# Differential attention with all keys of a slot in one run, token sums in two buffers, values one slot later and the output product in the middle of the next pair

## What is computed

```python
def _L1_attn_ref(x, Wq, Wk, Wv, Wo, lq1, lk1, lq2, lk2):
    h, dh = (16, 64)
    q = (x @ Wq).reshape(B, S, 2, h, dh)
    k = (x @ Wk).reshape(B, S, 2, h, dh)
    v = (x @ Wv).reshape(B, S, 2, h, dh)
    ...
    s1 = jnp.einsum('bshd,bthd->bhst', q1, k1) * scale
    s2 = jnp.einsum('bshd,bthd->bhst', q2, k2) * scale
    ...
    a1 = jax.nn.softmax(s1, axis=-1)
    a2 = jax.nn.softmax(s2, axis=-1)
    o = jnp.einsum('bhst,bthd->bshd', a1, v1) - lam * jnp.einsum('bhst,bthd->bshd', a2, v2)
    o = o.reshape(B, S, h * dh) * (1.0 - LAMBDA_INIT)
    return o @ Wo
x = _layernorm(x + _L1_attn_ref(x, ...), axis=-1)
```

## Time and profile before

| | us |
|---|---|
| three runs: lowest, median, highest | 1697.77, 1699.48, 1701.35 |
| the profiled execution: device time | 1697.64 |
| its span from first to last instruction | 1695.9 |
| PE busy in the span | 1608.2 (95%) |
| DVE, ACT, POOL busy in the span | 1187.9, 910.8, 676.7 (70%, 54%, 40%) |

### The profile page before, as it was taken

How to read it: one execution, slowest core, us unless ns; L and a number is a source line. 1 busy time by engine, 2 the same in 40 slices (tenths; PEclk the granted TensorE clock), 3 DMA queues, 4 the chain that set the end, 5 groups by cost and what they waited for, 6 DMA issues and landing times. The chain is left out here.

```text
span 1695.9 us, 51949 instructions
## 1 busy us (share of the span) xinstructions
PE 1608.2 (95%) x18158; PEld 1339.1 (79%) x18158; DVE 1187.9 (70%) x3418; ACT 910.8 (54%) x2619; POOL 676.7 (40%) x1070
## 2 busy tenths in 40 slices
PE   7998999897999999999999999899999999999695
PEld 5777788786777777777777777799999999999564
DVE  6888888675776677767676776467777777777654
ACT  5776777642454445444554454565655656565241
POOL 3665666411233333333333333234444344444346
PEclk9999999998999999999999999999999999999898
DMA  3213211121231000001110000112212212122231
GB/s 94 65 42 109 76 56 56 48 57 37 52 71 28 25 25 25 25 25 29 28 29 25 25 25 25 40 49 53 61 40 61 57 44 61 45 56 57 74 99 45
DMA packets 157654, 82.30 MB, mean 49 GB/s; under 512 B 17641, under 2 KB 153115, under 8 KB 157568
## 3 DMA queue, kind: packets, MB, share of 16 engines
q1 hardware_dynamic: 154800, 77.68, 17.2%
q0 software_dynamic: 2048, 3.15, 0.6%
q10 hardware_dynamic: 720, 0.33, 0.1%
HBM read 61.03 MB, written 21.27 MB: 49 GB/s over the span
## 5 line engine op out<-in xcount | busy, mean ns | idle before, releaser
L1437 PE MATMUL bank<-diff_xT,diff_w_score 128*128 128x128 f32 x2048 | 259.5, 280 | 0.8 <-ACT diff_xT L1549 0.8
L1437 PEld LDWEIGHTS bank<-diff_xT,diff_w_score 128*128 128x128 f32 x2048 | 242.1, 193 | 22.4 <-issue 20.2
L1556 ACT ACTIVATE diff_keys<-bank 128x512 f32<-128x512 f32 x256 | 152.4, 595 | 165.9 <-PE bank L1437 165.9
L1746 POOL TENSOR_TENSOR diff_prob<-diff_prob,diff_inv_sum 128x512 f32<-128x512 f32 x64 | 67.2, 1050 | 380.5 <-DVE diff_inv_sum L1649 380.5
L2225 POOL TENSOR_TENSOR lat_prob<-lat_prob,lat_inv_sum 128x512 f32<-128x512 f32 x128 | 133.5, 1043 | 208.3 <-DVE lat_inv_sum L2150 207.3
L2025 ACT ACTIVATE lat_prob<-bank,lat_neg_max 128x128 f32<-128x128 f32 x512 | 180.5, 372 | 1.0 <-DVE lat_neg_max L2170 1.0
L2036 ACT ACTIVATE lat_query<-bank 128x512 f32<-128x512 f32 x128 | 76.5, 597 | 174.4 <-PE bank L1920 174.4
L1950 PE MATMUL bank<-lat_catT,lat_query 128*128 128x128 f32 x1024 | 142.4, 282 | 3.9 <-ACT lat_query L2036 3.9
L1920 PE MATMUL bank<-lat_catT,lat_w_score 128*128 128x128 f32 x1024 | 139.5, 280 | 2.3 <-ACT lat_catT L2017 1.0
L1950 PEld LDWEIGHTS bank<-lat_catT,lat_query 128*128 128x128 f32 x1024 | 125.2, 193 | 15.8 <-issue 10.6
L1930 PE MATMUL bank<-lat_probT,lat_c_rep 32*128 32x256 f32 x2048 | 130.0, 391 | 3.1 <-DVE lat_z L2155 3.1
(11 more groups left out here) (273 smaller groups left out, 3656.6 us busy)
## 6 DMA issues: line engine op xcount, KB each, us to landing
lat_c_rep<-cat SPq DMA_DIRECT2D x128, 128.0 KB
stage<-low_y SPq DMA_DIRECT2D x64, 64.0 KB, 1.6
diff_x_rep<-stage SPq DMA_DIRECT2D x128, 32.0 KB, 1.8
lat_c_t<-cat SPq DMA_DIRECT2D x32, 128.0 KB, 2.2
exp_w<-in_L_ffn_w_dram SPq DMA_DIRECT2D x16, 256.0 KB, 3.0
expert_rows<-latw_zeros SPq DMA_DIRECT2D x4, 548.0 KB, 5.4
exp_rows<-expert_rows SPq DMA_DIRECT2D x8, 274.0 KB, 3.9
low_x_t<-in_x_dram SPq DMA_DIRECT2D x32, 64.0 KB, 1.9
```

The source lines that it names most:

```text
L1437: last = nc.tensor.matmul(ring[(k + d) % 2][:, j * P:(j + 1) * P], w_score[:, H1 * (k // 2) + HS * d + 4 * (k % 2) + j, :], xT[:, :], star ...
L1556: nc.scalar.activation(keys[:, k // 2, 4 * (k % 2):4 * (k % 2) + 4, :].rearrange("p h t -> p (h t)"), ring[(k + d) % 2][:, :], ACT.Copy).t ...
```

## The change

It reorders the work of a slot, and gives `mix` a second buffer. No matmul, copy or transfer is added or removed.

1. The four key banks of a slot stand in one run on PE; the mixes follow, then the values. On ACT the copies of banks 2 and 3 come before the copies of `mix`.
2. `mix` gets a leading dimension of 2, indexed by `d`. The values of slot `n - 3` run in slot `n`, where they were those of slot `n - 2`. They go into `ring[d]` as before, now with the heads of the other slot kind.
3. The output product moves from the end of slot d = 1 to the end of slot d = 0 of the following pair, from `ring[1]` to `ring[0]`. `z` moves to slot d = 1, and `y`, `lat` and their statistics and powers move by half a pair or more on DVE and POOL.
4. On DVE the copies of `mix` move behind the sums of the softmax (`mix_copies`), just ahead of the transpose (`turn`).
5. On SP the load of `x_rep` moves ahead of that of `x_res`; the stores of `y` and `lat` are for pair `i - 3`. One more round of `pair` drains the pipeline, and a transpose of a bias for the next phase uses `bank[1]` in place of `bank[0]`.

The core of the diff (the moves on DVE and POOL are cut to their heads):

```diff
-        mix = sb("mix", [P, 4, HS, 2, L])
+        mix = sb("mix", [P, 2, 4, HS, 2, L])
...
-            for i in range(NPAIR - 2, NPAIR + 2):
+            for i in range(NPAIR - 2, NPAIR + 3):
...
+                if have(i):
+                    wait(sp, mix_done, 2 * (i - 1))
+                    load_rep(i, par)
...
-                if have(i, 2):
-                    sp.wait_ge(y_done, i - 1)
-                    sp.dma_start(rows(x_out, i - 2), y[:, :]).then_inc(y_stored, 16)
-                if have(i, 2):
-                    sp.wait_ge(lat_done, i - 1)
-                    store_cat(i - 2, S, lat, lat_stored)
+                if have(i, 3):
+                    sp.wait_ge(y_done, i - 2)
+                    sp.dma_start(rows(x_out, i - 3), y[:, :]).then_inc(y_stored, 16)
+                if have(i, 3):
+                    sp.wait_ge(lat_done, i - 2)
+                    store_cat(i - 3, S, lat, lat_stored)
...
-                            tokens = mix[:, att:4 - att:3 - 2 * att, 2 * t + par, :, :].rearrange("p f b l -> p b f l")
+                            tokens = mix[:, d, att:4 - att:3 - 2 * att, 2 * t + par, :, :].rearrange("p f b l -> p b f l")
                             last = nc.tensor.matmul(
-                                ring[d][par * HD1:(par + 1) * HD1, t * P:(t + 1) * P]
+                                ring[1 - d][par * HD1:(par + 1) * HD1, t * P:(t + 1) * P]
...
+                    valued = have(i, 2) if d == 0 else have(i, 1)
                     if have(i):
                         if d == 0:
                             pe.wait_ge(xT_ready, i + 1)
-                            key_bank(n, d, 0, k_copied, 4 * n)
+                        key_bank(n, d, 0, k_copied, 4 * n)
+                        if d == 0:
+                            key_bank(n, d, 1, o_copied, n - 3)
+                        else:
                             key_bank(n, d, 1, z_done, i - 1)
-                        else:
-                            key_bank(n, d, 0, k_copied, 4 * n)
-                            key_bank(n, d, 1, o_copied, n - 2)
+                        key_bank(n, d, 2, k_copied, 4 * n + 1)
+                        key_bank(n, d, 3, k_copied, 4 * n + 2)
                     if have(i, 1):
                         pe.wait_ge(rep_loaded[1 - par], 32 * (i + par) if isinstance(i, int) else 32 * i + 32 * par)
                         mixes(n - 2, d, 1 - par)
...
-                    if have(i):
-                        key_bank(n, d, 2, k_copied, 4 * n + 1)
-                        key_bank(n, d, 3, k_copied, 4 * n + 2)
-                    if have(i, 1):
+                    if valued:
                         if have(i):
                             pe.wait_ge(k_copied, 4 * n + 3)
+                        elif d == 0:
+                            wait(pe, z_done, i - 2)
                         else:
-                            wait(pe, o_copied, n - 3)
-                        values(n - 2, d)
+                            wait(pe, o_copied, n - 4)
+                        values(n - 3, 1 - d)
...
-                    if d == 1 and have(i, 1):
-                        pe.wait_ge(o_copied, 2 * i)
+                    if d == 0 and have(i, 2):
+                        pe.wait_ge(o_copied, 2 * (i - 1))
                         for t in range(HS):
-                            last = nc.tensor.matmul(ring[1][:, 0:D], oT[:, t // 4, t % 4, :], wo[:, t, :],
+                            last = nc.tensor.matmul(ring[0][:, 0:D], oT[:, t // 4, t % 4, :], wo[:, t, :],
                                                     start=(t == 0), stop=(t == HS - 1))
                         last.then_inc(wo_done, 1)
...
+                    if have(i):
+                        copy_keys(n, d, 2)
+                        copy_keys(n, d, 3)
                     if have(i, 1):
                         act.wait_ge(mix_done, n - 1)
-                        wait(act, o_done, n - 2)
+                        wait(act, o_done, n - 3)
                         for q in range(2):
-                            nc.scalar.activation(mix[:, q % 2::2, :, q // 2, :],
+                            nc.scalar.activation(mix[:, d, q % 2::2, :, q // 2, :],
                                                  ps_mix[q][:, :].rearrange("p (f h l) -> p f h l", f=2, h=HS), ACT.Copy)\
                                 .then_inc(mix_act, 1)
                     if isinstance(i, int) and i == NPAIR:
                         latent.copies(act, (0, 1) if d == 0 else (4, 5))
-                    if have(i):
-                        copy_keys(n, d, 2)
-                        copy_keys(n, d, 3)
-                    if have(i, 1):
-                        act.wait_ge(o_done, n - 1)
-                        if d == 0:
+                    if have(i, 2) if d == 0 else have(i, 1):
+                        act.wait_ge(o_done, n - 2)
+                        if d == 1:
                             wait(act, wo_done, i - 1)
-                        nc.scalar.activation(oT[:, d, :, :].rearrange("p t e -> p (t e)"), ring[d][:, :], ACT.Copy)\
+                        nc.scalar.activation(oT[:, 1 - d, :, :].rearrange("p t e -> p (t e)"), ring[d][:, :], ACT.Copy)\
                             .then_inc(o_copied, 1)
...
+            def mix_copies(n, d):
+                dve.wait_ge(mix_done, n + 1)
+                wait(dve, o_done, n - 1)
+                for q in range(2, 4):
+                    nc.vector.tensor_copy(mix[:, d, q % 2::2, :, q // 2, :],
+                                          ps_mix[q][:, :].rearrange("p (f h l) -> p f h l", f=2, h=HS)).then_inc(mix_dve, 1)
+            def turn(n, d):
+                dve.wait_ge(p_done, 2 * (n + 1))
+                wait(dve, mix_done, n - 1)
+                nc.vector.transpose(probT[:, d, :], prob[:, d, :]).then_inc(pT_done, 1)
...
-                    if d == 0 and have(i, 2):
+                    if d == 0 and have(i, 3):
+                        dve.wait_ge(rstd_done[0], i - 2)
+                        wait(dve, y_stored, 16 * (i - 3))
+                        nc.vector.tensor_scalar(y[:, :], z[:, :], mean_var[:, 0, 0:1], rstd[:, 0:1], ALU.subtract,
+                                                ALU.mult).then_inc(y_done, 1)
+                    if d == 1 and have(i, 2):
                         dve.wait_ge(res_loaded, 16 * (i - 1))
                         dve.wait_ge(wo_done, i - 1)
-                        nc.vector.scalar_tensor_tensor(out=z[:, :], in0=ring[1][:, 0:D], scalar=1.0 - LAMBDA,
+                        nc.vector.scalar_tensor_tensor(out=z[:, :], in0=ring[0][:, 0:D], scalar=1.0 - LAMBDA,
                                                        in1=x_res[:, :], op0=ALU.mult, op1=ALU.add).then_inc(z_done, 1)
-                    if d == 1 and have(i, 2):
-                        dve.wait_ge(rstd_done[0], i - 1)
-                        wait(dve, y_stored, 16 * (i - 2))
-                        nc.vector.tensor_scalar(y[:, :], z[:, :], mean_var[:, 0, 0:1], rstd[:, 0:1], ALU.subtract,
-                                                ALU.mult).then_inc(y_done, 1)
+                    if d == 1 and have(i, 3):
+                        dve.wait_ge(rstd_done[1], i - 2)
+                        wait(dve, lat_stored, 32 * (i - 3))
+                        nc.vector.tensor_scalar(lat[:, :], y[:, :], mean_var[:, 1, 0:1], rstd[:, 1:2], ALU.subtract,
+                                                ALU.mult).then_inc(lat_n_done, 1)
...
+                    if have(i, 1):
+                        mix_copies(n - 2, d)
                     if done:
-                        dve.wait_ge(p_done, 2 * n)
-                        wait(dve, mix_done, n - 2)
-                        nc.vector.transpose(probT[:, 1 - d, :], prob[:, 1 - d, :]).then_inc(pT_done, 1)
+                        turn(n - 1, 1 - d)
...
-                        if have(i, 2):
-                            power(0, i - 1)
+                        if have(i, 3):
+                            power(1, i - 2)
                         if have(i):
                             power(2, i + 1)
                     else:
-                        if have(i, 2):
-                            power(1, i - 1)
+                        if have(i, 3):
+                            scale_shift(lat, 2, lat_n_done, lat_g_done, lat_done, i - 2)
                         if have(i):
                             scale_shift(ctx_n, 0, ctx_n_done, ctx_g_done, ctx_done, i + 1)
                         if have(i, 2):
-                            scale_shift(lat, 2, lat_n_done, lat_g_done, lat_done, i - 1)
+                            power(0, i - 1)
```

More of the change, by code:

```diff
@@ L1273, in products @@
         pe.wait_ge(self.r_loaded, 32)
-        nc.tensor.transpose(self.core.bank[0][:, 0:self.NB1], self.b1_raw[:, :], self.core.ident[0:self.NB1, 0:self.NB1])\
+        nc.tensor.transpose(self.core.bank[1][:, 0:self.NB1], self.b1_raw[:, :], self.core.ident[0:self.NB1, 0:self.NB1])\
```

(23 more changed lines are left out.)

15 lines of the change are left out of this document (6 added, 9 removed).

## The result

The changed kernel takes 1724.23 us (median of four runs, 1719.36 to 1728.32) against 1700.41 of the kernel before (1697.77 to 1702.05): 1.0143 times over the runs (the two medians alone give 1.0140), 95% interval 1.0116 to 1.0171. The profiled execution took 1719.36 us, its span is 1717.6 us, 21.7 us longer than that of before. The forecast was 1718, with 1708 to 1727 as its range.

What follows compares the result with a forecast made beforehand. PE was taken as the bound. Moved product +18.9, key run outrunning ACT +14.3, fewer shape changes -13.3, drain waits -1.3 sum to +18.6 us: median 1718 us against 1699.5, range 1708 to 1727.

Runs made afterwards that it cites:

- e7: Changed kernel with two `xT` buffers, exponentials behind key bank 1's copy, and the output product between key banks 1 and 2 of slot d = 1: 1687.21 us, 0.9932.
- e4: Kernel before the change with one of the output product's eight matmuls kept, so output is incomplete: 1704.32 us in one run, a loop pair still 19.98 us.
- e2: Changed kernel with key banks 2 and 3 put behind the mixes again, and their ACT copies likewise: 1722.34 us, 1.0115 of the kernel before.
- e3: Changed kernel with both exponentials on ACT placed behind the copy of key bank 1: 1722.99 us, 1.0117 of the kernel before.
- e5: The kernel of e4 with DVE taking `z` ahead of the softmax subtraction: 1659.6 us in one run, output still incomplete.

## What to carry over

An instruction group that is moved away takes its cover along: list what other engines do under it (here ACT's `xT` copy and DVE's `z`) and give each another cover or a second buffer before moving it. When a kernel's bound engine is busy all the time, its waits hide between starts; compare the distance of starts with the undisturbed pitch, and look in the warm-up for the order that the change will make. A group of the same weight shape is a cheap filler for a wait in a run: in e7 the product in the run of keys cost no change of shape and hid the copies.

## What the hardware showed

Changing the weights' shape costs PE start-to-start time: about 0.1 us to leave 128 x 128 weights (sixteen keys ahead of mixes 1.88 us, ahead of more keys 1.79), 0.1 us to enter them behind 32-row weights (0.38 against 0.28 for the first), 0.05 to enter 64-column ones (0.33 against 0.28). Taking 1.56 us of 19.97 from the engine that was busy 100% of the time changed nothing in the pairs of the loop (e4), since two waits of 0.22 and 0.86 us took its place, with the lengthened first keys.

The time from ACT's end to PE's start at the copy of `xT` was 0.05 us in the written-out pairs and 0.13 in the loop. I had expected the two to be alike. The changed kernel's trace has both, on either side of the loop's end: every pair of the loop starts its keys 0.13 behind the copy (751.20 to 751.33 in the rows above), and pair 30, the first behind the loop, 0.05 behind it (1020.07 + 0.28 = 1020.35 to 1020.40):

```profile
1020.07 0.28 ACT L1553 ACTIVATE diff_xT<-bank 128x128 f32<-128x128 f32 x1 [1.41 <-PE bank L1489]
1020.40 4.01 PE L1438 MATMUL bank<-diff_xT,diff_w_score 128*128 128x128 f32 x32 [0.37 <-ACT diff_xT L1553]
```

All six written-out pairs show 0.05 and all 26 pairs of the loop 0.13, in the changed kernel and likewise in e2, e3, e4 and e5. So the 0.08 us goes with the loop, where the semaphore counts come from registers, and not with the warm-up. Which part of the loop costs it (the counts from registers or something else) no run here separates.
